# Where an expert's weight is applied: once per expert tile instead of once per token row of the last part

## The reference

```python
B, T, D = 4, 1024, 256;  16 heads of 16;  8 experts, 2 chosen per token
xn = layernorm(x)
s  = attention(xn) @ o_w.T + o_b          # causal, with a decay by distance
probs = softmax(xn @ gate_w)
gate_score, gate_idx = top_k(probs, 2);  gate_score /= sum(gate_score)
combine = onehot(gate_idx) * gate_score * alpha      # weight of an expert for a token
y   = gelu(xn @ fc1_w[e] + fc1_b[e]) @ fc2_w[e] + fc2_b[e]
out = x + s * silu(sum over e of combine[t, e] * y[e, t])
```

## Time and profile before

| what | value |
|---|---|
| median of three runs (lowest to highest) | 763.61 us (763.34 to 765.75) |
| the profiled execution | 757.1 us |
| its span, as the trace has it | 755.3 us |
| PE busy in the span | 718.7 us (95%) |
| DVE busy | 577.6 us (76%) |
| ACT busy | 503.6 us (67%) |
| POOL busy | 243.5 us (32%) |
| packets of the DMA queue of SP | 94.5 MB, 56.7% of 16 engines' span |

### The profile page before, as it was taken

One profiled execution on the slowest core, in us unless ns is written; L12 is line 12 of the kernel. 1 busy time (PEld: TensorE's weight loads), 2 busy tenths in 40 slices (PEclk: granted clock), 3 DMA queues, 4 the chain that ended last, 5 costly groups with the idle time before them and its releaser, 6 DMA issues.

```text
span 755.3 us, 16299 instructions
## 1 busy us (share of the span) xinstructions
PE 718.7 (95%) x5079; PEld 414.1 (55%) x5082; DVE 577.6 (76%) x1817; ACT 503.6 (67%) x1036; POOL 243.5 (32%) x310
## 2 busy tenths in 40 slices
PE   7998997999999999999999999999999999999985
PEld 4554553434444444444444444444448999999864
DVE  5556988999999999999999999999424554444288
ACT  4785556666676676676676676677695666666374
POOL 1342234251213323323223323200005666666400
PEclk9999999999999999999999999999999999999999
DMA  7999935574684694695595696580179669865396
GB/s 187 278 181 287 248 134 164 63 100 81 112 137 107 120 179 103 122 176 113 113 168 119 117 164 123 108 127 15 34 187 230 198 173 235 196 217 176 105 391 252
DMA packets 85123, 119.62 MB, mean 158 GB/s; under 512 B 14031, under 2 KB 58575, under 8 KB 84975
## 3 DMA queue, kind: packets, MB, share of 16 engines
q1 hardware_dynamic: 76670, 94.54, 56.7%
q0 software_dynamic: 8368, 24.04, 11.0%
HBM read 72.61 MB, written 45.52 MB: 156 GB/s over the span
## 4 chain that ended last, share of the span: by engine, by line
PE 66%; DVE 18%; issue 7%; DMA 4%; POOL 1%; SPq 1%; ACT 1%; POOLq 0%; DVEq 0%
PE ps L1459 16%; PE ps L1396 13%; PE ps L1445 12%; DVE mxa L1013 9%; PE ps L1544 8%; PE ps L1566 8%; DVE ps L1008 4%; PE ps L1448 3%; DMA aug<-q_parts 3%; PE ps L1354 3%; PE ps L1527 2%; POOL arena L662 1%; DVE aug L1319 1%; DVE arena L1314 1%; DVE arena L1304 1%
## 5 line engine op out<-in xcount | busy, mean ns | idle before, releaser
L886 ACT ACTIVATE arena<-ps 128x512 f32<-128x512 f32 x576 | 298.3, 623 | 133.3 <-PE ps L1448 94.9
L1396 PE MATMUL ps<-aug 105*128 105x512 bf16 (+3 forms) x768 | 215.7, 329 | 13.5 <-DVE mxa L1008 6.8
L1445 PE MATMUL ps<-aug 108*128 108x512 bf16 (+3 forms) x768 | 206.2, 327 | 2.3 <-ACT arena L886 1.3
L1013 DVE TENSOR_REDUCE mxa<-ps 128x1 f32<-128x512 f32 x256 | 160.4, 680 | 12.4 <-PE ps L1396 12.3
L1459 PE MATMUL ps<-arena,v_q 128*32 128x512 f32 (+3 forms) x1536 | 140.4, 491 | 0.3
L1008 DVE CUSTOM_DVE_ANT_0 ps<-ps,blank,mxa 128x128 f32<-128x128 f32 (+3 forms) x256 | 126.6, 553 | 15.5 <-PE ps L1396 12.9
L1396 PEld LDWEIGHTS ps<-aug 105*128 105x128 bf16 x768 | 66.9, 97 | 129.1 <-DVE mxa L1008 45.7
L1008 DVE CUSTOM_DVE_ANT_0 ps<-ps,blank 128x128 f32<-128x128 f32 (+3 forms) x256 | 117.4, 523 | 7.1 <-PE ps L1396 4.5
L1448 PE MATMUL ps<-maskT_sb,idb 128*128 128x128 bf16 x512 | 112.4, 219 | 0.0
L1445 PEld LDWEIGHTS ps<-aug 108*128 108x128 bf16 x768 | 68.7, 97 | 48.3 <-ACT arena L886 18.5
L793 POOL DMA_INDIRECT y_dram<-arena,y_row_of x71 | 69.5, 978 | 53.9 <-DVE y_row_of L1244 46.0
(11 more groups left out here) (139 smaller groups left out, 728.3 us busy)
## 6 DMA issues: line engine op xcount, KB each, us to landing
aug<-k_parts SPq DMA_DIRECT2D x96, 128.0 KB, 6.8
aug<-q_parts SPq DMA_DIRECT2D x96, 128.0 KB, 7.1
arena<-xs_dram SPq DMA_DIRECT2D x71, 128.5 KB, 2.7
arena<-y_dram SPq DMA_DIRECT2D x16, 512.0 KB, 6.8
k_parts<-arena SPq DMA_DIRECT2D x16, 384.0 KB, 6.0
q_parts<-arena SPq DMA_DIRECT2D x16, 384.0 KB, 3.8
xn_dram<-arena SPq DMA_DIRECT2D x8, 512.0 KB, 7.3
a_dram<-arena SPq DMA_DIRECT2D x64, 64.0 KB
```

Of the source, the lines that this page charges most:

```text
L886: nc.scalar.activation(probs[SLOT[k, u]][:, half], score_bank(q, i), ACT.Exp).then_inc(exp_done, 1)
L1013: nc.vector.tensor_reduce(mxa[:, h:h + heads, col_], src, AX.X, ALU.max).then_inc(piece_used, 1)
L1396: ins = nc.tensor.matmul(out_, k_aug[n][0:SCORE_ROWS, h0 + h, ib * P:(ib + 1) * P], q_aug[n][0:SCORE_ROWS, h0 + h, lo:lo + width], start=T ...
L1445: ins = nc.tensor.matmul(out_, q_aug[n][0:ALL_ROWS, h, jb * P:(jb + 1) * P], k_aug[n][0:ALL_ROWS, h, i0:i0 + hi - lo], start=True, stop=lo ...
```

## The change

A row of the table carries one word more. Word 1 is the weight of the token for that expert; POOL copies it into `x_move` beside the row number, once for each of two choices in each of eleven windows. `take_row` takes both words out of a tile. After `y_evacuate` has written a tile, a new step `y_weigh` on DVE multiplies it in place by the weight column. `y_out` is now raised by `y_weigh`; `y_evacuate` raises a new semaphore, `y_added`, for which only `y_weigh` waits. In the last part `scale_first` is gone from ACT, and `add_second` is one plain addition over 512 columns, which waits for the load itself. The spare row for the table's unfilled rows has weight zero, the zero area is one word longer, and the arena four.

```diff
-W = D + 1
+W = D + 2
-        y_row_of = sb("y_row_of", [P, SLOTS], i32)
+        y_row_of = sb("y_row_of", [P, 2 * SLOTS], i32)
@@ POOL, windows 2 to 12
                     nc.gpsimd.tensor_copy(x_move[:, 0:count, 0:1].bitcast(i32),
                                           y_row[:, first_tile:first_tile + count, k:k + 1]).then_inc(rows_ready, 1)
-                    pool.wait_ge(rows_ready, 2 * r + k + 2)
+                    nc.gpsimd.tensor_copy(x_move[:, 0:count, 1:2],
+                                          weight[:, first_tile:first_tile + count, k:k + 1]).then_inc(rows_ready, 1)
+                    pool.wait_ge(rows_ready, 4 * r + 2 * k + 3)
@@ ACT, last part
-            in_turn(scale_first, silu)
+            for m in range(NT // 2):
+                silu(m)
@@ DVE, expert loop
-                nc.vector.tensor_copy(y_row_of[:, bass.ds(n, 1)], x_move[:, j % CH, 0:1].bitcast(i32)).then_inc(row_taken, 1)
+                nc.vector.tensor_copy(y_row_of[:, 2 * n:2 * n + 2], x_move[:, j % CH, 0:2].bitcast(i32)).then_inc(row_taken, 1)
-                nc.vector.tensor_tensor(ysb[j % STEP], bank(6 + j % 2)[:, 0:D], b2_sb[:, e, :], ALU.add).then_inc(y_out, 1)
+                nc.vector.tensor_tensor(ysb[j % STEP], bank(6 + j % 2)[:, 0:D], b2_sb[:, e, :], ALU.add).then_inc(y_added, 1)
+            def y_weigh(n, j):
+
+                dve.wait_ge(y_added, n + 1)
+                nc.vector.tensor_scalar(ysb[j % STEP], ysb[j % STEP], y_row_of[:, 2 * n + 1:2 * n + 2].bitcast(fp32), None,
+                                        ALU.mult).then_inc(y_out, 1)
-            skewed(((take_row, 3), (h_evacuate, 2), (y_evacuate, 0)), -CH)
+            skewed(((take_row, 3), (y_weigh, -1), (h_evacuate, 2), (y_evacuate, 0)), -CH)
+            y_weigh(SLOTS - 1, (SLOTS - 1) % STEP)
@@ DVE, last part
             def add_second(m):
                 j = m % DEEP
-                dve.wait_ge(y_scaled, m + 1)
-                for i in range(2):
-                    part = gsum[j][:, i * D:(i + 1) * D]
-                    ins = nc.vector.scalar_tensor_tensor(part, ya[m % DEEP_Y][:, i, 1, :], weight[:, 2 * m + i, 1:2],
-                                                         part, ALU.mult, ALU.add)
-                ins.then_inc(gsum_done, 1)
+                dve.wait_ge(ya_in[m % DEEP_Y], 16 * (m // DEEP_Y) + 16)
+                if m >= DEEP:
+                    dve.wait_ge(sg_done, m - DEEP + 1)
+                pair = ya[m % DEEP_Y]
+                nc.vector.tensor_tensor(gsum[j].rearrange("p (t d) -> p t d", d=D), pair[:, :, 0, :], pair[:, :, 1, :],
+                                        ALU.add).then_inc(gsum_done, 1)
```

More of the change, by code:

```diff
@@ L174, in is_last @@
     return isinstance(q, int) and q == NQ - 1
-def in_turn(ahead, what):
-    for m in range(AHEAD_OF_PRODUCT):
-        ahead(m)
-    for m in range(NT // 2):
-        what(m)
-        if m + AHEAD_OF_PRODUCT < NT // 2:
-            ahead(m + AHEAD_OF_PRODUCT)
 def attention_moe_kernel(nc, x, wqT, wkT, wvT, woT, qb, kb, vb, ob, gate, w1, b1, w2, b2, alpha,
@@ L237, in attention_moe_kernel @@
         tile_expert = sb("tile_expert", [P, SLOTS], i32)
-        y_row_of = sb("y_row_of", [P, SLOTS], i32)
+        y_row_of = sb("y_row_of", [P, 2 * SLOTS], i32)
         y_row = sb("y_row", [P, NT, 2], i32)
         blank = sb("blank", [P, W + P // 2])
-        zeros = blank[:, 1:W]
+        zeros, no_row = blank[:, 2:W], blank[:, 1:W]
         wide_mask = blank[:, :].bitcast(bf16)
@@ L246, in attention_moe_kernel @@
         spare = sb("spare", [P, E, 2], i32)
-        ARENA = 16 * 1024 + CH
+        ARENA = 16 * 1024 + 2 * CH
         arena = sb("arena", [P, ARENA])
@@ L303, in attention_moe_kernel @@
         at[0] = 0
-        xg = [x_move[:, j, 1:W] for j in range(CH)]
+        xg = [x_move[:, j, 2:W] for j in range(CH)]
         at[0] = len(TYPES[-1]) * T
@@ L390, in attention_moe_kernel @@
         g_done = sem("g_done"); w1_ready = sem("w1_ready"); l2_done = sem("l2_done")
-        y_out = sem("y_out"); y_stored = [sem(f"y_stored{n}") for n in range(STEP)]
+        y_out = sem("y_out"); y_added = sem("y_added"); y_stored = [sem(f"y_stored{n}") for n in range(STEP)]
         x_all_in = sem("x_all_in"); a_in = [sem(f"a_in{b}") for b in range(B)]
         ya_in = [sem(f"ya_in{n}") for n in range(DEEP_Y)]
-        vb_turned = sem("vb_turned"); vb_out = sem("vb_out"); vb_done = sem("vb_done"); ob_step = sem("ob_step"); ob_split = sem("ob_split"); s_proj = sem("s_proj"); y_scaled = sem("y_scaled")
+        vb_turned = sem("vb_turned"); vb_out = sem("vb_out"); vb_done = sem("vb_done"); ob_step = sem("ob_step"); ob_split = sem("ob_split"); s_proj = sem("s_proj")
         gsum_done = sem("gsum_done"); silu_done = sem("silu_done"); sg_done = sem("sg_done")
@@ L419, in many_zeros @@
         def many_zeros(n):
-            return bass.AP(zeros.tensor, zeros.offset, [list(zeros.ap[0]), [0, n], [1, D]])
+            return bass.AP(no_row.tensor, no_row.offset, [list(no_row.ap[0]), [0, n], [1, W - 1]])
         best, first, second, gap, gexp, where, norm, low = col
@@ L652, in _ @@
             pool.sem_inc(split_done, 8)
-            nc.gpsimd.memset(zeros, 0.0).then_inc(zeros_set, 1)
+            nc.gpsimd.memset(no_row, 0.0).then_inc(zeros_set, 1)
             for n in range(AUG):
@@ L765, in _ @@
                 first_tile, count = MOVES[r], MOVES[r + 1] - MOVES[r]
-                pool.dma_start(x_move[:, 0:count, 1:W], xn_t[:, first_tile:first_tile + count, :]).then_inc(x_moved, 16)
+                pool.dma_start(x_move[:, 0:count, 2:W], xn_t[:, first_tile:first_tile + count, :]).then_inc(x_moved, 16)
                 next_v(q, q % AUG)
@@ L794, in _ @@
                     out=y_dram, in_=ysb[n % STEP], in_offset=None,
-                    out_offset=bass.IndirectOffsetOnAxis(ap=y_row_of[:, n:n + 1], axis=0)).then_inc(y_stored[n % STEP], 16)
+                    out_offset=bass.IndirectOffsetOnAxis(ap=y_row_of[:, 2 * n:2 * n + 1], axis=0)).then_inc(y_stored[n % STEP], 16)
         @block.scalar
@@ L924, in _ @@
             nc.scalar.activation(std[:, :], veps[:, :], ACT.Silu)
-            def scale_first(m):
-                j = m % DEEP
-                act.wait_ge(ya_in[m % DEEP_Y], 16 * (m // DEEP_Y) + 16)
-                if m >= DEEP:
-                    act.wait_ge(sg_done, m - DEEP + 1)
-                for i in range(2):
-                    ins = nc.scalar.activation(gsum[j][:, i * D:(i + 1) * D], ya[m % DEEP_Y][:, i, 0, :], ACT.Identity,
-                                               scale=weight[:, 2 * m + i, 0:1])
-                ins.then_inc(y_scaled, 1)
             def silu(m):
```

## The result

The changed kernel takes 773.08 us (median of 4 runs, 770.58 to 777.42) against 764.46 for the kernel before on the same chip (4 runs, 763.34 to 765.75): ratio 1.0121, 95% interval 1.009 to 1.0152 (the quotient of the two medians is 1.0113). It is slower; 760.7 was forecast. Repeated on a second chip, beside more runs of before, the ratio is 1.0114 [1.0094, 1.0134] (768.15 against 759.62). So the change costs about 1.1%, 8.5 to 9 us, where 3 were to be gained. The profiled execution has 772.35 us, span 770.6, against 757.1 and 755.3.

What follows compares the result with a forecast made beforehand. PE was taken to bound the expert loop, DVE the last part with DMA also full. Gain 3.4 less loss 0.45 made 2.95 us, so 763.6 - 2.95 = 760.7 us, range 759.3 to 763.6.

Steps and rivals of the forecast that it cites:

- Part 1: Last part on DVE: period falls from 1.99 to 1.82 us and the start shortens by 1.3, gaining 3.4 us.
- the two bounds for an addition: Last part, 512-column addition on DVE: 0.69 us if nothing overlaps, 0.61 if it overlaps as its neighbours; 0.61 was taken.
- rival B: Last part bound by transfers, late loads eating the gain: gain only 0.5 to 2.2 us, time about 762; chance 0.19.
- rival D: More gain: y_weigh takes 0.28 us and PE, idle less before pair 4, keeps its clock; 0.5 to 1 more; chance 0.05.
- Part 2: End of the expert loop: y_weigh (0.41 us) lies on the serial piece and delays the last stores, losing 0.45 us.
- The harsher price: End of the expert loop: last two y_weigh would each push a POOL store beside them, losing up to 0.6 us more.
- Part 3: Middle of the expert loop: DVE has room for 0.41 us more per step, so cost 0, by a narrow margin.
- The ring: Expert loop, DVE's chain of waits from one y_evacuate to the next: 1.80 us against the 1.98 step, 0.18 to spare.
- Part 4: Attention windows and the rest: POOL's 22 copies of 0.19 us cost nothing, at worst 4.2; windows stay 27.95.
- A: Expert loop: register load waits until y_weigh finishes, DVE's chain takes 2.13 us against 1.98; time 771.3; chance 0.08.

Runs made afterwards that it cites:

- the two repetitions: Second profiles, on another chip, of the unedited kernel before (758.03 us in that run) and of the unedited changed kernel (768.15 us, ratio 1.0114).
- after_again: The changed kernel with no edit, timed again on a second chip beside the kernel before: 768.15 us, ratio 1.0114.
- late_reuse: Changed kernel with y_weigh behind h_evacuate, y_evacuate reusing the expert's number read two steps earlier, and PE waiting for y_added: 759.39 us, ratio 0.9997.
- weigh_late: Changed kernel with y_weigh(n-1) moved behind h_evacuate(n+2) on DVE, instead of ahead of it: 759.21 us, ratio 1.0002.
- no_weigh: Changed kernel without the multiplication by the weight; copies, long rows and new last part stay: 756.59 us, ratio 0.9973.
- weigh_psum: Changed kernel with y_weigh behind h_evacuate, reading the sum from PSUM and writing SBUF; the wait for y_stored moves to y_weigh: 759.6 us, ratio 1.0005.
- weigh_lag2: Changed kernel with y_weigh in the same place but weighing tile n-2 instead of n-1; PE still waits for y_out: 795.64 us, ratio 1.0483.
- pool_weigh: Changed kernel with the multiplication on GpSimd ahead of its store, expert's number reused, take_row early, PE waiting for y_added: 795.93 us, ratio 1.0464.
- lag2_bank: Changed kernel with y_weigh in the same place but weighing tile n-2, and PE waiting for y_added instead of y_out: 763.36 us, ratio 1.0036.

## Why the prediction was wrong

*Part 1, the last part: right.* The period is 1.80 for 1.82. By the old count, which takes the start of tile 68's `y_evacuate` as its fixed point (708.23 before, 726.42 after), the third `product` at 743.63 stands at 725.4, where 725.2 was forecast. Of the two bounds for an addition 0.60 held, though each shows 0.68 long: they overlap. Three first additions waited 8.8 us for loads, as the start was meant to; later none, so rival B did not happen. Of rival D the half about PE did: behind its pause ahead of pair 4 (3.52 us idle before, 1.85 after) the granted clock was 0.50 and 0.70 before (722 to 726; 0.50 is the lower of its two levels, 1.2 GHz) and 1.00 after (736 to 742). No gain from it shows, for DVE sets this part.

*Part 2, the end of the expert loop: right.* `y_weigh` took 0.35, between the bounds of 0.28 and 0.41. From the start of tile 68's `y_evacuate` to the last store it is 730.58 - 726.42 = 4.16 us, where the earlier trace rows have 711.94 - 708.23 = 3.71: 0.45 longer, the forecast loss (in the two repetitions 4.16 and 3.72):

```profile
726.42 0.42 DVE L1272 TENSOR_TENSOR arena<-ps,arena 128x256 f32<-128x256 f32 x1 [0.43 <-issue]
```

```profile
730.58 0.96 POOL L785 DMA_INDIRECT y_dram<-arena,y_row_of  x1 [0.34 <-issue]
```

Counted from the last `y_evacuate` it would seem that nothing was lost, 1.57 for 1.69. But the last three tiles now come 1.29 apart instead of 1.00, and the table books that in the loop. From the same fixed point to the end of the last addition the two parts together gave 44.52 - 41.57 = 2.95 us, the sum that was forecast (2.4 in the repetitions). The hit to the hundredth is luck; that both parts were sound is not.

The Trainium skill's "SBUF — State Buffer", section "Who interferes with whom", says that a DVE operation in a two-port mode and a GpSimd one on the shared pair lock each other out. The harsher price that the prediction took from it, a store of POOL pushed, hardly shows. The stores in the changed kernel (ns min/median/max):

```profile
L785 POOL DMA_INDIRECT y_dram<-arena,y_row_of x71: 958/967/1254, 579.8 to 730.6; - x71
```

Two of the 71 took 1.10 and 1.25, each with a y_weigh inside it (the same two in the repetition; before none is over 1.03); the others do not differ, those at the end either. The lock fits better on another pair: y_weigh and the normalise, 0.91 for 0.35, and no such thing from PSUM. By the rule I should have asked of every POOL operation in the loop; the price would have been about 1 us.

*Part 3, the middle of the expert loop: this step failed.* "The ring is 1.80 against 1.98: it fits with 0.18 to spare. ... Cost 0." The ring is 2.07. Its structure was right: which wait holds which load back stands there. What failed is the sum. From `y_evacuate` to `h_evacuate` I had 1.1, measured 1.22; from there back 0.7, measured 0.85. Missing was most of the gaps of 0.03 to 0.05 between each two pieces of the sequencer: nine on the way round, 0.38 in sum, and 0.05 and 0.03 ahead of the two loads, for all of which the sum had 0.25 (0.11 in its first half, 0.7 less 0.56 in its second). Missing too were the two assertions of 0.02 and the wait for `y_stored` with 0.02. By these rounded rows that is 0.27, all that the ring is over its forecast. I also took the 1.11 of the earlier trace rows as a sign that the first half fits; but in the earlier trace rows `h_evacuate` is released by PE, so that distance says nothing of what the sequencer needs. The excess over 1.98 is 0.10, and the prediction's own price for it, 0.7 us per 0.01, gives 7.2 over 70 steps.

The other 5.6 to 6.2 of the loop's 13 are not in that price. A loop that PE sets can catch up on DVE's side; one that DVE sets cannot. Before, the steps shorter than the median give back 4.1 us (both traces), after only 2.0; and what is late adds in full. The register loads show it. They take 0.30 in the median but now and then far more. That is no more frequent by the change (8 of 142 are over 0.36 in both profiles of before and in the first of after, 12 in after_again), but now each one counts. In after_again, the trace of L1268 and DVE's timeline around it:

```profile
L1268 DVEq TENSOR_LOAD <-tile_expert x1: 795/795/795, 629.6 to 629.6; - x1
```

```profile
628.34 0.43 DVE L1272 TENSOR_TENSOR arena<-ps,arena 128x256 f32<-128x256 f32 x1 [0.62 <-issue]
...
630.90 0.42 DVE L1272 TENSOR_TENSOR arena<-ps,arena 128x256 f32<-128x256 f32 x1 [0.92 <-issue]
```

The load is 0.49 longer, and so is the step (2.57 for 2.08). In late_reuse a load of 0.77 leaves the step at 1.98. The steps over the median by more than 0.08 are 8 to 10 before, 18 and 21 after. How those 6 us divide between such loads, the clash (1.0) and late x tiles is not settled. The runs cut the loop's 13 in another way: 8.8 to 9.8 go with y_weigh's place (to weigh_late's 142.4), so more than the 7.2 hang on the order; 1.9 go with the multiplication (to no_weigh's 140.6); 1.2 to 2.8 are left without it (to 139.4 and 137.8), in single profiles.

*Part 4: right.* no_weigh and weigh_late have the copies and windows of 27.95; the 22 new copies took 0.19 each.

*The rivals.* Of A the outcome happened: DVE's ring broke, with 0.27 of extra latency where 0.18 decided. Its mechanism did not: the register load does not wait until `y_weigh` has finished, it starts 0.01 behind `y_weigh`'s start (714.42 and 714.41). The extra latency came from the gaps and small pieces. That 771.3 was named and 773.1 measured is luck: A had 10.7 for the ring and nothing else, where 7.2 for the ring and some 6 beside it were measured. A had a chance of 0.08, for a margin of 0.18 in a sum of some ten parts, of which several came from no row. A margin thinner than the number of unpriced gaps times one gap is not a margin; near to even odds would have been right.

*What is left.* With the ring mended the change is worth nothing: weigh_late 1.0002, late_reuse 0.9997, weigh_psum 1.0005. Without the multiplication it is 0.9973. So the weighing costs in the loop about what it saves in the last part, even where DVE's ring has room. In the one profile of each, weigh_late against no_weigh: loop +1.9 (0.8 of it in the last three steps, where tiles come each 1.3 instead of 1.0), last weigh +0.4, tail -0.8. No version that does the whole work beats the kernel before by more than the intervals; all but weigh_lag2 and pool_weigh beat the changed one.

## What to carry to other kernels

When an instruction with a semaphore wait is put ahead of a register load, everything of that load that used to run beside the awaited work moves behind it; add up the ring round the engine with every sequencer piece and the gap after it, from a stretch in which the sequencer is the releaser and not from one in which PE is. Here a spare of 0.18 in 1.98 on paper was an excess of 0.10 on the chip. With so thin a spare, put the waiting instruction where its wait is already over: the order was worth 1.1%, the instruction itself 0.3%. And after moving the raiser of a semaphore, look for every other engine that waits for it: weigh_lag2 was 4.8% slower than before, and lag2_bank, which differs from it only in what PE waits for, 0.4%.

## What the runs showed of the hardware

- A register read on DVE's sequencer is 0.30 for the load, 0.19 and 0.07 of arithmetic and 0.02 for the assertion, with gaps of 0.03 to 0.05: about 0.8 from the start of the load to the start of the instruction that uses it (715.2 to 716.02 in the ring above, with one wait in it that was met, at 0.02).
- Single loads took up to 0.81 (weigh_late). The long ones are not spread evenly: of weigh_late's loads that began 0.25 to 0.7 us ahead of one of POOL's scatters, 29 of 51 took over 0.36, of those that began over 0.9 ahead, 4 of 74 (late_reuse: 34 of 54, and 1 of 7). Why is open. With PE setting the pace most of them cost nothing: late_reuse has 37 such loads and a median step of 1.98.
- Without a wait ahead of it, a register load began 0.06 behind the start of `y_evacuate` (641.22 and 641.28); behind an instruction that waits, it began only when that wait was over (714.37 and 714.4).
- A TENSOR_SCALAR over 128x256 fp32 with a column of scalars took 0.35 from SBUF to SBUF and 0.475 from PSUM; on GpSimd 0.93.
- Beside a GpSimd TENSOR_TENSOR (0.73) it took up to 0.92 from SBUF (0.97 in the repetition) and 0.475 unchanged from PSUM. The copy of two words (L1227) took 0.50 to 0.78 in six of 71 cases instead of 0.16.
- DVE instructions of 512 columns, each shown as 0.68, follow each other every 0.60.
